# Two-layer transformer on one core: the second layer's causal mask in four quarters, its by-query scores one pair earlier, VectorE's and GpSimd's work in another order

## What is computed

```python
x = _layernorm(x + _L0_attn_ref(...)); x = _layernorm(x + _L0_ffn_ref(...))
# _L1_attn_ref: HEADS, D_MODEL, D_V = 16, 128, 64; D_K = 8
scores = jnp.einsum('bhqd,bhkd->bhqk', q, k) / scale
causal = jnp.triu(jnp.ones((T, T), dtype=bool), k=1)
scores = jnp.where(causal, -jnp.inf, scores)
ctx = jnp.einsum('bhqk,bhkd->bhqd', jax.nn.softmax(scores, axis=-1), v)
out = ctx.transpose(0, 2, 1, 3).reshape(B, T, HEADS * D_V) @ Wo
```

## Time and profile before

| | us |
|---|---|
| median of 3 runs (lowest, highest) | 951.15 (950.95, 953.62) |
| profiled execution, its own time | 950.26 |
| its span, first to last instruction | 948.5 |
| second layer's attention | about 385 to 845 |
| maxima busy, L1375, 128 times | 122.5 |
| by-query masks busy, L1113, 256 times | 50.4 |

### The profile page before, as it was taken

The page is one execution under the profiler, slowest core; times in us unless marked ns, Lnnn a source line. Parts: engine busy times, 40 slices in busy tenths (PEclk is TensorE's granted clock), DMA queues, the critical chain, the costliest instruction groups (busy, mean ns, idle before and its releaser), DMA issues. The chain is left out here.

```text
span 948.5 us, 19520 instructions
## 1 busy us (share of the span) xinstructions
PE 790.8 (83%) x7061; PEld 451.7 (48%) x7061; DVE 575.1 (61%) x1715; ACT 472.5 (50%) x750; POOL 296.2 (31%) x437
## 2 busy tenths in 40 slices
PE   1588989998829999179999999999999999739970
PEld 0234444444316778125555555555555555534430
DVE  4458999999531111244576776666666656324687
ACT  0377888887812222035454545445455444306664
POOL 3012333333336000424344444434443322100152
PEclk9989999999958999679999999999999999878995
DMA  0274333433215553221454444333334332210002
GB/s 26 72 239 124 97 89 96 108 84 89 69 32 129 158 149 88 67 59 45 96 96 96 96 96 92 74 86 78 81 76 96 79 85 51 56 45 0 1 0 89
DMA packets 111705, 78.02 MB, mean 82 GB/s; under 512 B 12272, under 2 KB 103088, under 8 KB 111616
## 3 DMA queue, kind: packets, MB, share of 16 engines
q1 hardware_dynamic: 107984, 71.16, 30.5%
q0 software_dynamic: 3344, 5.56, 2.2%
q10 hardware_dynamic: 288, 0.13, 0.1%
HBM read 37.86 MB, written 13.63 MB: 54 GB/s over the span
## 5 line engine op out<-in xcount | busy, mean ns | idle before, releaser
L1375 DVE TENSOR_REDUCE l_neg_max<-l_by_query 128x6 bf16<-128x768 f32 x128 | 122.5, 957 | 129.9 <-PE l_by_query L1121 129.6
L1447 POOL TENSOR_SCALAR_AFFINE_SELECT l_probs<-l_probs 128x512 f32<-128x512 f32 x128 | 87.1, 680 | 190.9 <-ACT l_probs L1250 190.7
L493 ACT ACTIVATE l_probs<-l_ps_s,minus_bound 128x1024 f32<-128x1024 f32 x128 | 137.9, 1116 | 2.3 <-PE l_ps_s L367 1.4
L1250 ACT ACTIVATE l_probs<-l_by_key 128x768 f32<-128x768 f32 x128 | 103.8, 811 | 68.1 <-PE l_by_key L1151 63.9
L1166 PE MATMUL l_ps_c<-l_probs,l_values 128*64 128x256 f32 (+1 forms) x1024 | 113.5, 343 | 0.0
L1166 PEld LDWEIGHTS l_ps_c<-l_probs,l_values 128*64 128x64 f32 x1024 | 62.9, 138 | 39.7 <-issue 21.2
L1190 PE MATMUL l_ps_v<-w_o,l_ctx 128*128 128x128 f32 x512 | 68.6, 290 | 15.1 <-DVE l_ctx L1393 15.1
L382 PE MATMUL l_ps_o<-l_probs,l_vpad 128*32 128x256 f32 x1024 | 80.6, 397 | 0.2
L1103 PE MATMUL l_ps_v<-w_v,l_xT 128*128 128x512 f32 x128 | 72.8, 651 | 0.4 <-ACT l_values L1271 0.2
L1190 PEld LDWEIGHTS l_ps_v<-w_o,l_ctx 128*128 128x128 f32 x512 | 62.6, 200 | 20.9 <-DVE l_ctx L1393 15.5
L1271 ACT ACTIVATE l_values<-l_ps_v 128x512 f32<-128x512 f32 x64 | 38.2, 597 | 65.4 <-PE l_ps_v L1103 60.0
(11 more groups left out here) (229 smaller groups left out, 1422.5 us busy)
## 6 DMA issues: line engine op xcount, KB each, us to landing
l_rrep<-rden_d SPq DMA_DIRECT2D x32, 512.0 KB
q_ring<-l_parts SPq DMA_DIRECT2D x192, 64.0 KB
k_ring<-l_parts SPq DMA_DIRECT2D x192, 64.0 KB
w<-in_L_ffn_w_dram SPq DMA_DIRECT2D x32, 256.0 KB, 3.0
disp_d<-zeros SPq DMA_DIRECT2D x8, 320.0 KB, 3.7
l_xin<-in_L_attn_x_dram SPq DMA_DIRECT2D x16, 128.0 KB, 3.1
l_xr<-in_L_attn_x_dram SPq DMA_DIRECT2D x16, 128.0 KB, 2.5
x_d<-l_x SPq DMA_DIRECT2D x16, 128.0 KB, 2.1
```

The source lines that it names most:

```text
L493: act.activation(probs[c % RING][:, :], ps_s[c % 2][:, :], ACT.Exp, bias=k["minus_bound"][:, :], scale=SCALE).then_inc(probs_sb, 1)
L1250: act.activation(probs[c % P_RING][:, :, 0:N + P], by_key[:, :, 0:N + P], ACT.Exp, scale=SCALE).then_inc(p_sb, 1)
L1375: dve.tensor_reduce(neg_max[:, :, half, :, h].rearrange("p a u -> p u a"), by_query[:, :, 0:3 * P].rearrange("p u (a q) -> p u a q", a=3), ...
L1447: pool.affine_select(out=corners, in_=corners, compare_op=ALU.is_ge, fill=0.0, base=0, pattern=[[0, 4], [1, P]], channel_multiplier=-1).th ...
```

## The change

1. The mask matmuls use a smaller constant `corner` (128 by 256, the upper and lower 64 partitions hold the same triangle) and four quarters of the array: for each head one matmul of 64 rows by 64 columns that streams 256 columns into query rows 0 to 63, and one that streams 128 columns into query rows 64 to 127 (the other 128 need no mask there). Two whole-array matmuls become four quarter ones.
2. In `step`, every by-query block moves one cycle ahead: pair 2 of batch b + 1 ends cycle 0, pairs 0 and 1 of batch b + 2 end cycles 6 and 7. `maxima_by_head` of the first half moves from cycle 4 to cycle 3, right behind `denominators`. `x_by_channel` moves from the head of cycle 0 to behind its `context`.
3. ScalarE: `x_out` follows the exponential of cycle 0, `high_part` moves from the end of cycle 1 to behind the exponential of cycle 2, `maxima_out` moves with its matmul.
4. VectorE: `maxima` one pair on; `add_attention`, `lower_parts` and `third_input` each about a cycle later, `add_expert` and `second_input` from cycles 1 and 3 to cycles 6 and 7. GpSimd: `gather` from cycle 3 to cycle 5, `root` for batch b + 3 from cycle 1 to cycle 6, behind the gather.

```diff
                     for u in two:
-                        pe.matmul(by_query[:, u, P:3 * P], ident_bf[:, :], k["causal"][:, 0:2 * P],
+                        r = slice(64 * u, 64 * u + 64)
+                        pe.matmul(by_query[0:64, u, P:3 * P], ident_bf[r, r], k["corner"][r, :],
+                                  start=True, stop=False, skip_group_check=True)
+                    for u in two:
+                        r = slice(64 - 64 * u, 128 - 64 * u)
+                        later = by_query[64:128, u, P:3 * P].rearrange("p (a k) -> p a k", k=P)[:, :, 64:P]
+                        pe.matmul(later, ident_bf[r, r], k["corner"][r, :].rearrange("p (a k) -> p a k", k=P)[:, :, 0:64],
                                   start=True, stop=False, skip_group_check=True)
...
             def step(b):
-                x_by_channel(b + 2)
                 scores_by_key(b, 2)
                 context(b, 0)
-                scores_by_query(b + 1, 1)
+                x_by_channel(b + 2)
+                scores_by_query(b + 1, 2)
...
                 reciprocals(b - 1)
+                maxima(b + 1, 2)
+
                 add_attention(b - 2)
...
                 maxima(b + 1, 7)
+
+                add_expert(b + 3)
                 maxima(b + 2, 0)
+
+                second_input(b + 3)
+                maxima(b + 2, 1)
...
                 mask(b, 7)
+                gather(b + 4)
                 mask(b + 1, 0)
+                root(pow2, x2_step, (b + 3) * X2 + 3 * NB, mv2, veps2, rstd2, b + 3)
                 mask(b + 1, 1)
```

More of the change, by code:

```diff
@@ L146, in _ @@
             pool.memset(k["tri_bf"][:, :], 1.0).then_inc(filled, 1)
-            pool.memset(k["causal"][:, :], 0.0).then_inc(filled, 1)
+            pool.memset(k["corner"][:, :], 0.0).then_inc(filled, 1)
             pool.iota(iota_base[:, :], pattern=[[CAP, E]], base=0, channel_multiplier=0).then_inc(filled, 1)
@@ L157, in _ @@
                                base=0, pattern=[[1, P]], channel_multiplier=-1).then_inc(cut, 1)
-            pool.affine_select(out=k["causal"][:, :].rearrange("p (a b) -> p a b", b=P),
-                               in_=k["causal"][:, :].rearrange("p (a b) -> p a b", b=P),
-                               compare_op=ALU.is_ge, fill=-1e30,
-                               base=0, pattern=[[0, 4], [-1, P]], channel_multiplier=1).then_inc(cut, 1)
+            pool.wait_ge(cut, 2)
+            for half in range(2):
+                rows = k["corner"][64 * half:64 * half + 64, :].rearrange("p (a b) -> p a b", b=P)
+                pool.affine_select(out=rows, in_=rows, compare_op=ALU.is_ge, fill=-1e30,
+                                   base=0, pattern=[[0, 2], [-1, P]], channel_multiplier=1).then_inc(cut, 1)
         @block.tensor
@@ L1214, in step @@
                 denominators(b, 1)
+                maxima_by_head(b + 1, 0)
                 values_of(b + 1, 1)
-                scores_by_query(b + 1, 4)
+                scores_by_query(b + 1, 5)
                 scores_by_key(b, 6)
                 context(b, 4)
-                maxima_by_head(b + 1, 0)
                 values_of(b + 1, 2)
-                scores_by_query(b + 1, 5)
+                scores_by_query(b + 1, 6)
                 scores_by_key(b, 7)
@@ L1285, in step @@
             def step(b):
+                exponential(b, 2)
                 x_out(b + 2)
-                exponential(b, 2)
                 exponential(b, 3)
                 context_out(b, 0)
+                exponential(b, 4)
                 high_part(b + 2)
-                exponential(b, 4)
                 values_out(b + 1, 0)
@@ L1407, in step @@
                 reciprocals(b - 1)
+                maxima(b + 1, 2)
                 add_attention(b - 2)
[L1409 to L1412 removed]
+                maxima(b + 1, 3)
+                lower_parts(b + 2)
+                maxima(b + 1, 4)
                 third_input(b - 2)
[L1415 to L1419 removed]
+                maxima(b + 1, 5)
                 divide(b - 1, 0)
                 divide(b - 1, 1)
[L1423 removed]
+                maxima(b + 1, 6)
                 divide(b - 1, 2)
                 divide(b - 1, 3)
[L1427 removed]
                 maxima(b + 1, 7)
+                add_expert(b + 3)
                 maxima(b + 2, 0)
+                second_input(b + 3)
+                maxima(b + 2, 1)
             steps(step)
@@ L1467, in step @@
                 mask(b, 2)
+                mask(b, 3)
                 root(pow3, x3_step, (b - 2) * X3 + 1 + 2 * NB, mv3, veps3, rstd3, b - 2)
-                mask(b, 3)
-                root(pow2, x2_step, (b + 3) * X2 + 3 * NB, mv2, veps2, rstd2, b + 3)
                 mask(b, 4)
@@ L1882, in program @@
             "tri_bf": sb("tri_bf", [P, P], BF16), "ones_bf": sb("ones_bf", [P, P], BF16),
-            "ones": sb("ones", [P, P], FP32), "causal": sb("causal", [P, 4 * P], BF16),
+            "ones": sb("ones", [P, P], FP32), "corner": sb("corner", [P, 2 * P], BF16),
             "zeros": sb("zeros", [P, 5 * C], FP32), "minus_half": sb("minus_half", [P, 4], FP32),
```

24 lines of the change are left out of this document (7 added, 17 removed).

## The result

The changed kernel takes 952.98 us (median of 20 runs), the kernel before 949.84 us (20 runs beside it). The ratio is 1.0035, 95% interval 1.0018 to 1.0051: 1.7 to 4.8 us slower, best guess 3.3. The forecast was 3.9; its 955.0 us stood on 951.15, the median of three earlier runs of the kernel before. The bound of 0.3% lies inside the interval, so "slightly slower" is shown, "slower by over 0.3%" is not.

A forecast was written before the change was run, and what follows sets the result against it. Bound: the loop through SyncE's ring transfers, not TensorE's sum. Loops + 4.2 (13 of + 0.32), start + 1.0, end - 1.3 gave + 3.9 us; on 951.15 us, forecast 955.0 us, range 947.5 to 961.

The forecast's parts named there:

- First part, + 0.35: Loop from cycle 7's last by-query matmuls to SyncE's first ring transfer: 7.05 instead of 6.70 us, behind the later high part.
- The mask, 0.26: Quarter mask up to the next shape: exposed weights 0.05, stream 0.11, leaving 0.09, starts 0.01; entering behind whole-array adds 0.09 us.
- rival B: The quarters' weights hide behind the switch: mask 0.21 us, + 0.16 us per batch, about 952.6 us; chance 0.25.
- A: The forecast itself: the loop through SyncE stays the bound and grows, 955.0 us; chance 0.42.
- Second part, no change: Loop from the first ring transfer to cycle 6's by-key scores: same twelve transfers and rows, no change, +-0.3 us per batch.
- third part, - 0.03: Loop's cycles 6 and 7: mask 0.04 dearer in cycle 6, 0.06 cheaper in cycle 7, - 0.03 us with rounding.
- TensorE's sum: TensorE alone, per batch: cycles 1 to 6 + 0.24, cycle 7 - 0.06, cycle 0 - 0.18, `maxima_by_head` - 0.09; - 0.1 us.
- Start, + 1.0: Pipeline start: root behind the gather fills the first ring 1.3 us later, second ring delayed too; + 1 us, bounds 0 and + 4.
- C: Quarters that write one bank run in turn: mask 0.31 us, + 0.48 us per batch, 957.5 us; chance 0.10.
- D: No drain between quarters and halves, weights hide: mask 0.11 us on the loop, - 0.13 per batch, about 948.2 us; chance 0.13.
- F: The start costs its upper bound of + 4 us: 958 us in total; chance 0.05.
- E: The long ring transfer takes 0.6 instead of 1.34 us: - 0.42 us per batch, about 945 us; chance 0.05.

The follow-up runs named there:

- e5: The changed kernel with SyncE sending the rows of maxima of pairs 0 to 3 behind the first six ring transfers instead of all twelve; 939.9 us, ratio 0.9898.
- e6: The kernel before with SyncE sending the rows of maxima of pairs 0 to 3 behind ten ring transfers instead of twelve; 940.0 us, ratio 0.9912.
- e1: The changed kernel with ScalarE's high part moved back to the end of cycle 1, ahead of the exponential of cycle 2; ratio 1.0042.
- e10: The changed kernel with one more, unused transfer per batch on SyncE between the wait for the high part and the first ring transfer; ratio 1.0128.
- e7: e5 with the whole-array mask of the kernel before instead of the quarters; ratio 0.9926.
- e4: The changed kernel with GpSimd's root of batch 0 ahead of the gather again, in step -3 only; ratio 1.0035.
- e2: The kernel before with the four quarter masks alone, no order changed; 948.04 us, ratio 0.9994.
- e3: The changed kernel with the whole-array mask of the kernel before, so the new order alone; 951.25 us, ratio 1.0044.
- e8: e6 with the mask on four quarters, order otherwise that of before; ratio 0.9944.

## Why the prediction was right, point by point

**The bound.** Right. The loop through SyncE sets the period of both kernels (e5, e6: -0.99 and -0.45 us a batch when only the rows are issued earlier). Of the two views that disagreed, TensorE busy 49.5 of 50 us and a wait that comes in nearly every batch, the second was the one to follow.

**First part, + 0.35.** The mechanism and nearly the size: median + 0.25 (6.95 against 6.70), mean over 13 batches + 0.36 (7.03 against 6.67). Moving the high part back (e1) takes the 0.25 away. That this term reached the period is argued and not shown: in e1 neither the period nor the total fell, while e10, with a delay at the same place, lengthened the period by as much as the delay.

**The mask, 0.26.** It measured 0.23 (602.20 to 602.42 in rounded times; 0.229 us in nearly every block of the ten profiles with quarters). Of its pieces the switch on entering (0.09 forecast, 0.093 in e5 against e7) and the quarters side by side held; the exposed weights were mis-sized. I took 0.05 from fp32 weights of L1166; with the switch of 0.09 on leaving and a stream of 0.11, 0.03 is left for weights and four starts together, where I had 0.06. The value lies between rival B's 0.21 and A's 0.26. By the Trainium skill's rule that a change of the tiling mode drains TensorE (TensorEngine Tiling (Array Packing), Tiling Modes) entering the quarters costs a switch, and the 0.093 us agree. Its rule under Restrictions, that column tiling gives up the fast weight load, is not contradicted, but its price here is at most the 0.03 us that is left.

**Second part, no change, and third part, - 0.03.** The second measured 10.94 against 11.05 on average, inside the 0.3 that I had left; the third 7.84 against 7.93, since the mask is cheaper. Loop sum: forecast + 0.32, measured + 0.10 over 12 batches and + 0.15 over 13. By the means of the three parts, + 0.36, - 0.11 and - 0.09, the first gave what was forecast; what is missing is 0.06 at the masks of cycles 6 and 7, which were mis-sized, and 0.11 in the second part, a drift that this noise doesn't tell from nothing.

**The wait ahead of cycle 6, 0.9.** Measured 0.97 (11.6 us in 12 times). A wait is the loop less the engine's own work; the loop grew by less than I said and TensorE's sum shrank by more (below), so that the number fits is partly luck.

**TensorE's sum, - 0.1 us a batch.** Wrong in size: - 0.44 (e5 against e6), of which 0.08 is e6's rest of the wait for the rows, so - 0.36. The step that failed is the mask of cycles 1 to 6: not dearer by 0.24 but by about 0.05 in all (six times 0.093 for entering against 0.085 saved). The other terms were near: cycle 7 gives 0.10 (forecast 0.06), cycle 0 0.20 (0.18), `maxima_by_head` 0.11 (0.09). Most of this did not move the time of this change, because it lies beside the loop; it would have misled me on e5.

**Start, + 1.0.** Measured + 2.2. The root's part was right, the first by-query block comes 1.3 us later (21.86 against 20.57 behind the gather) and e4 gives it back. The second ring is later by 2.8 us, not 1.3 (29.21 against 26.39). My step that "the wait for the rows that was there anyway has taken the rest" failed: the first reciprocals inherit most of it. How much is uncertain: before and e2, which differ in the mask alone, have 64.6 and 62.7, and the seven profiles of the new order with its start untouched 66.2 to 68.0. Where the rows of maxima are issued as in before, the new order's start is 3.1 us longer on average (after, e1, e3 against before, e2); where they are issued early, 5.6 us (e5, e7 against e6, e8). That is three times the forecast or more.

**End, - 1.3.** Measured - 1.8 in this pair of profiles. Over all of them the middle one of the ten profiles of the new order is 66.6, that of the four of the old order 67.8: - 1.3.

**The sum, + 3.9.** Measured 3.3, or 2.4 in this pair of profiles. The forecast named the right bound and the right direction, but that the number fits is partly luck: the loops gave half of their 4.2 us and the start at least twice its 1.0.

**The rivals.** B had the mask and with it the loop (+ 0.16 forecast, + 0.10 to + 0.15 measured), A the mechanism and, through a start that cost more, the sum. C (quarters in turn, 0.31) and D (no switch, 0.11) are excluded by 0.23. F, a start at its upper bound of + 4, is half borne out: + 2.2 in this pair, more over all profiles. E did not come: a long transfer still stands among the twelve.

**Left open.** What of the start's loss belongs to which piece of VectorE's and GpSimd's order. The long transfer of SyncE's queue (0.7 to 2.2 us instead of 0.6, in about two of three batches, at a drifting place; the twelve take 7.6 to 9.2 us) is nearly explained. The trace of before has a packet of 16 KB on a DMA queue for instructions from 615.19 to 616.54 us, and the ring transfer issued at 615.58 ends at 616.92, 0.38 behind it. In the fourteen profiles, from 450 to 775 us, 112 ring transfers hold the queue for over 0.7 us, and 109 of them end 0.36 to 0.44 us behind the end of an instruction packet. That SyncE waits there for its own instructions is the reading that fits; no run takes the packets away.

## What to carry to other kernels

Where a wait on the bound engine comes back in every round, follow it around the loop: here two short transfers issued six places earlier in SyncE's queue were worth 1.4% of the changed kernel (e5) and two places earlier 0.9% of the kernel before (e6), while the change that shortened TensorE's work by 0.36 us a batch gained nothing. Before an engine is relieved or work is respread, look in the issue queue for what is ready early and sent late. And price the start and the end of a pipeline as carefully as its period: in e5 the new order lost at the start most of what it won in the batches and at the end. A wait in the rows of the weight load is not yet a cost; compare what the step ahead of it takes with and without it.

## What the hardware showed that I had not expected

- The four quarter matmuls (64 rows by 64 columns, two streams of 256 columns and two of 128) start within 0.01 us of each other and cost 0.23 us to the next shape, of which 0.09 is the switch. Two of them, from different rows of the array, write different partitions of the same buffer (`by_query[:, u]`) at that moment, and the rows show no price for it. The Trainium skill (TensorEngine Tiling (Array Packing), Restrictions and Gotchas) says that different row tiles cannot access the same PSUM bank simultaneously; if the two had run in turn, the streams would be 0.11 + 0.05 us and the mask about 0.28 by my estimate, which the measured 0.23 does not bear out.
- The switch costs the same 0.09 us from the whole array into quarters as from the whole array into halves, so a mask cut finer saves its stream (0.11 us) and pays it back on entering, unless the step ahead is not on the whole array either (cycle 7).
- Spread: the layer begins between 383.9 and 390.7 us in programs whose code up to there is the same but for a constant, and one transfer in two of three batches takes up to 3.7 times as long as its neighbours (2.2 us in e6). Terms under 0.15 us a batch can't be told from one profile.
